# A recurrent layer between two feed-forward layers: POOL's normalisation ahead of inject, TensorE's gates ahead of the next transposes, and a negated mean that is added

## The chip, the cores and the metric

The kernel runs on one core of a Trainium2 chip. The metric is the device time in microseconds of one execution. The engines are named as in the profile: PE (TensorE, the matrix engine; PEld are its weight loads), DVE (VectorE), ACT (ScalarE), POOL (GpSimd) and SP, which only issues DMAs here.

## The reference

The input x has 32 x 256 rows of 128 features. Three layers follow, each with a layer norm and a residual:

```python
def _layernorm(x, axis=-1, eps=1e-05):
    m = jnp.mean(x, axis=axis, keepdims=True)
    v = jnp.var(x, axis=axis, keepdims=True)
    return (x - m) / jnp.sqrt(v + eps)
...
x = x + 0.5 * _L0_ffn_ref(_layernorm(x, axis=-1), L0_ffn_w_up, L0_ffn_w_down)
x = x + _L0_attn_ref(_layernorm(x, axis=-1), L0_attn_Wf, L0_attn_Wi, L0_attn_Wh)
x = x + 0.5 * _L0_ffn_ref(_layernorm(x, axis=-1), L0_ffn_w_up, L0_ffn_w_down)
```

The FFN is two linear layers with weights of -1, 0 and 1 (128 to 512 features and back) with a gelu between them; each divides its input by its root mean square first. The middle layer is a gated recurrence over the 256 positions of a sequence: with f and i the sigmoids of x Wf and x Wi, and g a positive function of x Wh, it computes h[t] = f[t] h[t-1] + i[t] g[t] from h = 0.5, in the reference by way of logarithms and an associative scan.

## The kernel before

The 8192 rows are held in SBUF as `X`, 64 tiles of 128 rows, and worked on in 16 groups of four tiles. The three layers run one after the other, each over the 16 groups, so there are 48 group steps, n = 0 to 47: n below 16 is the first FFN, 16 to 31 the recurrent layer, 32 to 47 the second FFN. Every engine has one queue with an order written out by hand, and semaphores between them. An instruction that waits holds up all that stands behind it on its engine.

**Each group of each layer begins alike.** DVE computes mean and variance of the rows (`stats`, `mean_var`, into `mv`). POOL makes the scale: for an FFN in `ln_roots`, for two groups at a time (L176 and L178 two small tensor_scalars, L180 a square root as a power, L183 an add), of which DVE takes the reciprocal `rstd` (L500); for the recurrent layer in `rnn_scales` (L188, L191), one group at a time. Then POOL's `norm` (L201) writes the normalised rows to `xn` with four instructions of 128x128: subtract the mean, multiply by rstd, both of them per-partition scalars. `xn` has two buffers; `norm(n)` waits until group n-2 is transposed. TensorE's `turn(n)` (L333) transposes the four tiles into the one PSUM buffer `T`, and waits until T was taken for the group before.

**FFN.** ACT and DVE take T apart into two float16 halves `xt_hi` (L259) and `xt_lo` (L504). TensorE multiplies with the up weights (L351, L352), ACT applies gelu (L263) and makes `h_hi` (L269), DVE makes `h_lo` (L508) and `h_half` (L516). `gram` (L368, L373, L374) gives the sums of squares on a diagonal, which DVE reads out as `ssq` (L521); POOL's `rms_step` (L208, L211) makes the root of it; DVE takes the reciprocal (`scale_y`, L525) and `add_ffn` (L532) adds the down product `Y` (L386) to X.

**Recurrent layer**, group r (n = 16 + r). ACT copies T to `xt` (`copy_turned`, L275; two buffers). `gates(r)` on TensorE (L401) makes three products of 512 columns in float32, each of them two records in the trace. ACT's `gate(r, n)` (L282) applies the sigmoid to each: `sig_h`, `sig_i`, and f in place. DVE's `candidate` (L540) makes `cand` from the first, POOL's `inject_step` (L219) multiplies it by sig_i, DVE's `scan` (L550) runs the recurrence into `hidden`, TensorE's `turn_back` (L410) transposes that into PSUM, and DVE's `add_rnn` (L556) adds it to X. The queues are ordered by a step s, which on POOL and DVE goes over all layers, with r = s - 16:

- POOL in step s: inject(r), rnn_scales(s - 12), norm(s + 2), then ln_roots and rms_step where there are any
- DVE in step s: scan(r - 1), candidate(r), stats and mean_var for the second FFN of group r - 2 and for the recurrent layer of group s - 11, add_rnn(r - 1)
- ACT in step r: the copy of group r + 1, then the three sigmoids of group r
- TensorE in step r: turn of group r + 1, gates(r), turn_back(r - 1)

Of the kernel before, what the change touches and what calls it, by code (L numbers as in the profile page):

```python
# [8 lines left out]
ALU = mybir.AluOpType  # L9
# [3 lines left out]
P = 128  # L13
# [9 lines left out]
def build_macaron(nc, x_in, w_f, w_i, w_h, w_up, w_down, x_out):  # L23
# [3 lines left out]
    tiles = batch * seq // P  # L27
    groups = tiles // TILES
# [7 lines left out]
    with ExitStack() as ctx:  # L36
        def sb(name, shape, dt=F32):
            return ctx.enter_context(nc.sbuf_tensor(name, shape, dt))
# [22 lines left out]

        st = sb("st", [P, 3, 2, TILES, 6])
        mv = [sb(f"mv{l}", [P, tiles, 2]) for l in range(3)]
        rstd = [sb(f"rstd{l}", [P, tiles]) for l in range(3)]
        var_eps = [sb(f"var_eps{l}", [P, 2, 4 * TILES]) for l in range(3)]
        root = [sb(f"root{l}", [P, 2, 4 * TILES]) for l in range(3)]
# [56 lines left out]
        def cols(g, n=TILES):  # L123
            return slice(g * TILES, g * TILES + n)
# [26 lines left out]
        @block.gpsimd  # L151
        def _(pool):
            eng = nc.gpsimd
            eng.memset(ident[:], 0.0).then_inc(ident_zero, 1)
            eng.memset(ones[:], 1.0).then_inc(consts_set, 1)
            eng.memset(half[:], 0.5).then_inc(consts_set, 1)
            eng.memset(minus_half[:], -0.5).then_inc(consts_set, 1)
            pool.wait_ge(ident_zero, 1)
            eng.affine_select(out=ident[:], in_=ident[:], compare_op=ALU.not_equal, fill=1.0, base=0,
                              pattern=[[-1, P]], channel_multiplier=1).then_inc(consts_set, 1)  # L160

            def gram_constants():
                eng.memset(ident16[:], 0.0).then_inc(ident_zero, 1)
                eng.memset(off_diag[:], OFF_DIAGONAL).then_inc(ident_zero, 1)
                pool.wait_ge(ident_zero, 3)
                eng.affine_select(out=ident16[:], in_=ident16[:], compare_op=ALU.not_equal, fill=1.0, base=0,
                                  pattern=[[-1, P]], channel_multiplier=1).then_inc(consts_set, 1)
                eng.affine_select(out=off_diag[:], in_=off_diag[:], compare_op=ALU.not_equal, fill=0.0, base=0,
                                  pattern=[[0, TILES], [-1, P]], channel_multiplier=1).then_inc(consts_set, 1)

            def ln_roots(i, l, first, n):

                w, par, s = n * TILES, i % 2, XN_SPLIT ** -2
                var = mv[l][:, cols(first, w), 1]
                pool.wait_ge(mv_done[l], i + 1)
                eng.tensor_scalar(var_eps[l][:, par, 0:w], var, s * RMS_EPS ** 2, LN_EPS * s * RMS_EPS ** 2,  # L176
                                  ALU.mult, ALU.add).then_inc(var_set[l], 1)
                eng.tensor_scalar(var_eps[l][:, par, w:2 * w], var, s, 1.0, ALU.mult, ALU.mult).then_inc(var_set[l], 1)  # L178
                pool.wait_ge(var_set[l], 2 * (i + 1))
                eng.tensor_tensor(root[l][:, par, 0:2 * w], var_eps[l][:, par, 0:2 * w], half[:, 0:2 * w],  # L180
                                  ALU.pow).then_inc(root_done[l], 1)
                pool.wait_ge(root_done[l], i + 1)
                eng.tensor_tensor(den[l][:, par, 0:w], root[l][:, par, 0:w], root[l][:, par, w:2 * w],  # L183
                                  ALU.add).then_inc(den_done[l], 1)

            def rnn_scales(g):
                pool.wait_ge(mv_done[1], g + 1)
                eng.tensor_scalar(var_eps[1][:, g % 2, 0:TILES], mv[1][:, cols(g), 1], 1.0, LN_EPS,  # L188
                                  ALU.mult, ALU.add).then_inc(var_set[1], 1)
                pool.wait_ge(var_set[1], g + 1)  # L190
                eng.tensor_tensor(rstd[1][:, cols(g)], var_eps[1][:, g % 2, 0:TILES], minus_half[:],  # L191
                                  ALU.pow).then_inc(rstd_done[1], 1)

            def norm(n):
                l, g = divmod(n, groups)
                pool.wait_ge(rstd_done[l], link_of(l, g) + 1)
                if n >= 2:
                    pool.wait_ge(xt_ready, n - 1)
                for t in range(TILES):
                    c = g * TILES + t  # L200
                    m = eng.tensor_scalar(xn[:, n % 2, t, :], X[:, c, :], mv[l][:, c, 0:1], rstd[l][:, c:c + 1],  # L201
                                          ALU.subtract, ALU.mult)
                m.then_inc(xn_ready, 1)

            def rms_step(F):
                par = F % 2
                pool.wait_ge(ssq_done, F + 1)
                eng.tensor_tensor(rms[:, par, :], ssq[:, par, :], half[:, 0:TILES], ALU.pow).then_inc(rms_ready, 1)  # L208
                pool.wait_ge(rms_ready, F + 1)

                eng.tensor_scalar(rms_den[:, par, :], rms[:, par, :], 2.0 * (2.0 / dff) ** 0.5, 2.0 * H_SPLIT * RMS_EPS,  # L211
                                  ALU.mult, ALU.add).then_inc(rms_den_done, 1)

            def inject_step(g):
                pool.wait_ge(cand_done, g + 1)
                pool.wait_ge(sig_done, 3 * g + 2)
                if g >= 2:
                    pool.wait_ge(scan_done, g - 1)
                eng.tensor_tensor(inject[:, g % 2, :], sig_i[:, g % 2, :], cand[:, g % 2, :], ALU.mult).then_inc(inject_done, 1)  # L219

            ln_roots(0, *links(0)[0])
            norm(0)
            ln_roots(1, *links(0)[1])
            gram_constants()
            norm(1)
            ln_roots(2, *links(0)[2])
            for s in range(0, 3 * groups):
                k, r, q = s, s - groups, s - 2 * groups
                if 0 <= r < groups:
                    inject_step(r)  # L230
                if 0 <= s - 12 < groups:
                    rnn_scales(s - 12)
                if s + 2 < 3 * groups:
                    norm(s + 2)
                if k + 4 < groups and k % 2 == 1:
                    ln_roots(link_of(0, k + 3), *links(0)[link_of(0, k + 3)])
                if 0 <= s - 28 < groups and s % 2 == 0:
                    ln_roots((s - 28) // 2, *links(2)[(s - 28) // 2])
                if 0 <= k - 1 < groups:
                    rms_step(k - 1)  # L240
                if 0 <= q - 1 < groups:
                    rms_step(q - 1 + groups)
            rms_step(2 * groups - 1)

        @block.scalar
        def _(act):
            eng = nc.scalar
# [29 lines left out]
            def gate(g, n):  # L277
                act.wait_ge(gate_ready, 3 * g + n + 1)
                if n == 1 and g >= 2:
                    act.wait_ge(inject_done, g - 1)  # L280
                out = (sig_h[:, g % 2, :], sig_i[:, g % 2, :], Z[g % 2][2])[n]
                eng.activation(out, Z[g % 2][n], ACT.Sigmoid).then_inc(sig_done, 1)  # L282
# [23 lines left out]
                ffn(k, k + 1)  # L306
            act.preload_act_table(ACT.Sigmoid)
            for r in range(groups):
                if r + 1 < groups:
                    turned(groups + r + 1)  # L310
                for n in range(3):
                    gate(r, n)
            act.preload_act_table(ACT.Gelu)
            turned(2 * groups)
            for k in range(groups):
# [3 lines left out]
        def _(pe):  # L319
# [8 lines left out]
            def turn(n):  # L328
                pe.wait_ge(xn_ready, n + 1)
                if n >= 1:  # L330
                    pe.wait_ge(xt_taken, n)
                for t in range(TILES):
                    m = pe.transpose(T[:, t * P:(t + 1) * P], xn[:, n % 2, t, :], ident[:])  # L333
                m.then_inc(xt_ready, 1)
# [68 lines left out]
            def turn_back(g):  # L403
                pe.wait_ge(scan_done, g + 1)
                if g == 0:
                    pe.wait_ge(ssq_done, groups)
                else:
                    pe.wait_ge(rnn_added, g)
                for t in range(TILES):
                    m = pe.transpose(O[:, t, :], hidden[:, g % 2, t * P:(t + 1) * P], ident[:])  # L410
                m.then_inc(turned_back, 1)
# [20 lines left out]
            gram(groups - 1)  # L432
            down(groups - 1)
            for r in range(groups):
                turn(groups + r + 1)
                gates(r)
                if r >= 1:
                    turn_back(r - 1)
            up(groups, 0)
            turn(2 * groups + 1)  # L440
            up(groups, 1)
# [192 lines left out]
```

## Time and profile before

| | |
|---|---|
| median of 3 runs | 420.42 us (419.04 to 420.66) |
| the profiled execution | 420.15 us, span 417.7 us |
| mean granted TensorE clock | 0.894 of full speed |
| POOL busy | 292.7 us (70%), 385 instructions |
| PE busy | 293.7 us (70%), 2701 matmuls |
| DVE busy | 276.3 us (66%) |
| ACT busy | 183.9 us (44%) |

The span runs from the first to the last instruction; what lies around it makes up the rest of the execution's time. A busy share is an average over the three layers, so the stages have to be read apart. Matmuls overlap one another in the records: their starts, not the sum of their lengths, tell how fast they went. Times in a timeline are in microseconds from the start of the span. A row with "xN" has merged N like instructions that followed one another.

### The profile page before, as it was taken

Reading aid. Unit: us, or ns where it says so; the run is one execution under the profiler, and the core shown is the slowest. Engines: PE = TensorE matmul, PEld = TensorE weight load, DVE = VectorE, ACT = ScalarE, POOL = GpSimd, SP = SyncE. Lnnn points to the kernel's source line nnn. Section 1 sums busy time; section 2 is a strip of 40 time slices with the busy share of each in tenths; the row PEclk is TensorE's granted clock in tenths of the full one; section 3 lists DMA queues with packets and bytes.
Section 4 is the critical chain, followed back from the end, with each engine's and each line's share of the span. In section 5 each row is a group of like instructions: output and inputs, shape, how many; then the busy total and the mean of one; then the engine's idle time right before and its main releaser. Section 6 shows DMA issues by size and latency. Waiting matters only on the chain. (4 is left out here: it accounts for less than half of the span.)

```text
span 417.7 us, 7376 instructions
## 1 busy us (share of the span) xinstructions
PE 293.7 (70%) x2701; PEld 205.5 (49%) x2701; DVE 276.3 (66%) x827; ACT 183.9 (44%) x230; POOL 292.7 (70%) x385
## 2 busy tenths in 40 slices
PE   1549988998898445555446555455679889888994
PEld 1228776777677222222223222222258668666874
DVE  5469999999898254444444443242578977887995
ACT  1257757575655212222222222222386656665670
POOL 4997988898896655545554445575798889888722
PEclk9969999999999786678886668877799999999999
DMA  6900000000000000000000000000000101110111
GB/s 200 271 0 2 2 2 3 2 2 2 2 2 2 0 2 0 0 0 0 2 1 0 1 0 0 0 0 0 3 0 27 52 27 31 48 52 27 53 52 50
DMA packets 18035, 9.57 MB, mean 23 GB/s; under 512 B 592, under 2 KB 17872, under 8 KB 18000
## 3 DMA queue, kind: packets, MB, share of 16 engines
q1 hardware_dynamic: 16896, 8.39, 7.3%
q10 hardware_dynamic: 1104, 0.72, 0.6%
q8 instruction: 21, 0.34, 0.3%
q14 instruction: 14, 0.11, 0.1%
HBM read 4.92 MB, written 4.19 MB: 22 GB/s over the span
## 5 line engine op out<-in xcount | busy, mean ns | idle before, releaser
L201 POOL TENSOR_SCALAR xn<-X,mv,rstd 128x128 f32<-128x128 f32 x192 | 152.5, 808 | 3.0 <-DVE rstd L500 0.9
L263 ACT ACTIVATE U<-U 128x1024 f32<-128x1024 f32 x64 | 65.6, 1025 | 79.5 <-PE U L352 79.5
L333 PE MATMUL T<-ident,xn 128*128 128x128 f32 x192 | 37.8, 331 | 77.3 <-POOL xn L201 77.3
L508 DVE SCALAR_TENSOR_TENSOR h_lo<-U,h_hi 128x1024 f16<-128x1024 f32 x64 | 77.6, 1213 | 1.9 <-ACT h_hi L269 1.9
L219 POOL TENSOR_TENSOR inject<-sig_i,cand 128x512 f32<-128x512 f32 x16 | 20.3, 1268 | 74.1 <-DVE cand L540 38.1
L351 PE MATMUL U<-xt_hi,up_w 128*128 128x512 f16 x128 | 51.0, 398 | 29.7 <-DVE h_lo L508 23.3
L333 PEld LDWEIGHTS T<-ident,xn 128*128 128x128 f32 x192 | 27.3, 168 | 90.4 <-POOL xn L201 85.1
L269 ACT ACTIVATE h_hi<-U 128x1024 f16<-128x1024 f32 x64 | 65.9, 1030 | 1.0
L540 DVE SCALAR_TENSOR_TENSOR cand<-U,sig_h 128x512 f32<-128x512 f32 x16 | 11.0, 686 | 76.2 <-ACT sig_h L282 76.2
L386 PE MATMUL Y<-down_w,h_hi 128*128 128x128 f16 x512 | 60.6, 219 | 0.0
L386 PE MATMUL Y<-down_w,h_lo 128*128 128x128 f16 x512 | 60.6, 219 | 0.0
L374 PE MATMUL G<-h_lo,h_hi 128*128 128x128 f16 x512 | 60.6, 219 | 0.0
L373 PE MATMUL G<-h_half,h_hi 128*128 128x128 f16 x512 | 60.6, 219 | 0.0
L374 PEld LDWEIGHTS G<-h_lo,h_hi 128*128 128x128 f16 x512 | 50.1, 98 | 3.8
L373 PEld LDWEIGHTS G<-h_half,h_hi 128*128 128x128 f16 x512 | 50.1, 98 | 3.4
L208 POOL TENSOR_TENSOR rms<-ssq,half 128x4 f32<-128x4 f32 x32 | 32.7, 1021 | 25.9 <-DVE ssq L521 25.9
L352 PE MATMUL U<-xt_lo,up_w 128*128 128x512 f16 x128 | 50.5, 394 | 0.0
L386 PEld LDWEIGHTS Y<-down_w,h_lo 128*128 128x128 f16 x512 | 50.1, 98 | 0.0
L386 PEld LDWEIGHTS Y<-down_w,h_hi 128*128 128x128 f16 x512 | 50.1, 98 | 0.0
L275 ACT COPY xt<-T 128x512 f32<-128x512 f32 x16 | 9.4, 587 | 89.4 <-PE T L333 89.4
L180 POOL TENSOR_TENSOR root<-var_eps,half 128x16 f32<-128x16 f32 (+1 forms) x17 | 47.3, 2782 | 1.4
L401 PE MATMUL U<-xt,gate_w 128*128 128x512 f32 x64 | 48.1, 895 | 0.0
(66 smaller groups left out, 416.5 us busy)
## 6 DMA issues: line engine op xcount, KB each, us to landing
X<-in_L_attn_x SPq DMA_DIRECT2D x16, 256.0 KB, 5.2
out_x<-X SPq DMA_DIRECT2D x16, 256.0 KB, 2.3
up_raw<-in_L_ffn_w_up ACTq DMA_DIRECT2D x1, 256.0 KB, 4.1
down_raw<-in_L_ffn_w_down ACTq DMA_DIRECT2D x1, 256.0 KB, 4.9
gate_raw<-in_L_attn_Wh ACTq DMA_DIRECT2D x1, 64.0 KB, 4.5
gate_raw<-in_L_attn_Wi ACTq DMA_DIRECT2D x1, 64.0 KB, 4.3
gate_raw<-in_L_attn_Wf ACTq DMA_DIRECT2D x1, 64.0 KB, 4.2
```

The lines of the kernel that those rows point to most:

```text
L180: eng.tensor_tensor(root[l][:, par, 0:2 * w], var_eps[l][:, par, 0:2 * w], half[:, 0:2 * w], ALU.pow).then_inc(root_done[l], 1)
L201: m = eng.tensor_scalar(xn[:, n % 2, t, :], X[:, c, :], mv[l][:, c, 0:1], rstd[l][:, c:c + 1], ALU.subtract, ALU.mult)
L263: eng.activation(U[part][:], U[part][:], ACT.Gelu, scale=1.0 / XN_SPLIT).then_inc(gelu_done, 1)
L269: eng.mul(h_hi[:, F % 2, 2 * part:2 * part + 2, :], U[part][:], H_SPLIT).then_inc(h_hi_done, 1)
L333: m = pe.transpose(T[:, t * P:(t + 1) * P], xn[:, n % 2, t, :], ident[:])
L351: pe.matmul(U[part][:, c, :], up_w[:, f0:f0 + P], xt_hi[:, F % 2, :], start=True, stop=False)
L352: m = pe.matmul(U[part][:, c, :], up_w[:, f0:f0 + P], xt_lo[:, F % 2, :], start=False, stop=True)
L373: pe.matmul(G[:, t, :], hi, half_, start=False, stop=False)
L374: m = pe.matmul(G[:, t, :], hi, lo, start=False, stop=(t == TILES - 1 and c == chunks - 1))
L386: m = pe.matmul(Y[:, par, t, :], part[:, par, c, t * P:(t + 1) * P], down_w[:, c, :], start=(c == 0 and part is h_hi), stop=(c == chunks - ...
L401: pe.matmul(Z[g % 2][n], gate_w[:, n, :], xt[:, g % 2, :], start=True, stop=True).then_inc(gate_ready, 1)
L508: vec.scalar_tensor_tensor(out=h_lo[:, F % 2, 2 * part:2 * part + 2, :], in0=U[part][:], scalar=H_SPLIT, in1=h_hi[:, F % 2, 2 * part:2 * p ...
```

## The change

Three things change. First, for every group of every layer POOL computes the negated mean into a new buffer `neg_mean` with one more small tensor_scalar (in `ln_roots` and in `rnn_scales`), and `norm` adds it instead of subtracting the mean; the number it waits for on `var_set` rises accordingly. Second, in POOL's loop norm(s + 2) comes first in a step, ahead of inject_step and rnn_scales. Third, in the recurrent layer TensorE issues gates(r) and turn_back(r - 1) ahead of the turn of group r + 1, and ACT issues the three sigmoids of group r ahead of the copy of group r + 1.

```diff
--- before.py
+++ after.py
@@ -61,6 +61,7 @@
 
         st = sb("st", [P, 3, 2, TILES, 6])
         mv = [sb(f"mv{l}", [P, tiles, 2]) for l in range(3)]
+        neg_mean = [sb(f"neg_mean{l}", [P, tiles]) for l in range(3)]
         rstd = [sb(f"rstd{l}", [P, tiles]) for l in range(3)]
         var_eps = [sb(f"var_eps{l}", [P, 2, 4 * TILES]) for l in range(3)]
         root = [sb(f"root{l}", [P, 2, 4 * TILES]) for l in range(3)]
@@ -176,7 +177,9 @@
                 eng.tensor_scalar(var_eps[l][:, par, 0:w], var, s * RMS_EPS ** 2, LN_EPS * s * RMS_EPS ** 2,
                                   ALU.mult, ALU.add).then_inc(var_set[l], 1)
                 eng.tensor_scalar(var_eps[l][:, par, w:2 * w], var, s, 1.0, ALU.mult, ALU.mult).then_inc(var_set[l], 1)
-                pool.wait_ge(var_set[l], 2 * (i + 1))
+                eng.tensor_scalar(neg_mean[l][:, cols(first, w)], mv[l][:, cols(first, w), 0], -1.0, 1.0,
+                                  ALU.mult, ALU.mult).then_inc(var_set[l], 1)
+                pool.wait_ge(var_set[l], 3 * (i + 1))
                 eng.tensor_tensor(root[l][:, par, 0:2 * w], var_eps[l][:, par, 0:2 * w], half[:, 0:2 * w],
                                   ALU.pow).then_inc(root_done[l], 1)
                 pool.wait_ge(root_done[l], i + 1)
@@ -187,7 +190,9 @@
                 pool.wait_ge(mv_done[1], g + 1)
                 eng.tensor_scalar(var_eps[1][:, g % 2, 0:TILES], mv[1][:, cols(g), 1], 1.0, LN_EPS,
                                   ALU.mult, ALU.add).then_inc(var_set[1], 1)
-                pool.wait_ge(var_set[1], g + 1)
+                eng.tensor_scalar(neg_mean[1][:, cols(g)], mv[1][:, cols(g), 0], -1.0, 1.0,
+                                  ALU.mult, ALU.mult).then_inc(var_set[1], 1)
+                pool.wait_ge(var_set[1], 2 * (g + 1))
                 eng.tensor_tensor(rstd[1][:, cols(g)], var_eps[1][:, g % 2, 0:TILES], minus_half[:],
                                   ALU.pow).then_inc(rstd_done[1], 1)
 
@@ -198,8 +203,8 @@
                     pool.wait_ge(xt_ready, n - 1)
                 for t in range(TILES):
                     c = g * TILES + t
-                    m = eng.tensor_scalar(xn[:, n % 2, t, :], X[:, c, :], mv[l][:, c, 0:1], rstd[l][:, c:c + 1],
-                                          ALU.subtract, ALU.mult)
+                    m = eng.tensor_scalar(xn[:, n % 2, t, :], X[:, c, :], neg_mean[l][:, c:c + 1], rstd[l][:, c:c + 1],
+                                          ALU.add, ALU.mult)
                 m.then_inc(xn_ready, 1)
 
             def rms_step(F):
@@ -226,12 +231,12 @@
             ln_roots(2, *links(0)[2])
             for s in range(0, 3 * groups):
                 k, r, q = s, s - groups, s - 2 * groups
+                if s + 2 < 3 * groups:
+                    norm(s + 2)
                 if 0 <= r < groups:
                     inject_step(r)
                 if 0 <= s - 12 < groups:
                     rnn_scales(s - 12)
-                if s + 2 < 3 * groups:
-                    norm(s + 2)
                 if k + 4 < groups and k % 2 == 1:
                     ln_roots(link_of(0, k + 3), *links(0)[link_of(0, k + 3)])
                 if 0 <= s - 28 < groups and s % 2 == 0:
@@ -306,10 +311,10 @@
                 ffn(k, k + 1)
             act.preload_act_table(ACT.Sigmoid)
             for r in range(groups):
+                for n in range(3):
+                    gate(r, n)
                 if r + 1 < groups:
                     turned(groups + r + 1)
-                for n in range(3):
-                    gate(r, n)
             act.preload_act_table(ACT.Gelu)
             turned(2 * groups)
             for k in range(groups):
@@ -432,10 +437,10 @@
             gram(groups - 1)
             down(groups - 1)
             for r in range(groups):
-                turn(groups + r + 1)
                 gates(r)
                 if r >= 1:
                     turn_back(r - 1)
+                turn(groups + r + 1)
             up(groups, 0)
             turn(2 * groups + 1)
             up(groups, 1)
```

## Rows read from the trace of the kernel before

**Rows 1.** Windows: width, busy us (xinstructions) of PE PEld DVE ACT POOL, PEclk, DMA, GB/s

```profile
36.00:132.00 96.00, 86.17 (x1079) 68.25 (x1078) 90.93 (x266) 62.82 (x71) 84.00 (x112) 1.00 0.01 2
139.00:300.00 161.00, 85.03 (x210) 42.93 (x210) 66.76 (x265) 36.59 (x61) 89.61 (x110) 0.76 0.00 0
...
220.00:224.00 4.00, 3.73 (x8) 2.18 (x9) 0.24 (x1) 1.18 (x2) 0.22 (x1) 0.50 0.00 0
```

**Rows 2.** Timeline, POOL: start us, us, engine, line, operation, out<-in, [idle before <-releaser]

```profile
138.87 1.27 POOL L219 TENSOR_TENSOR inject<-sig_i,cand 128x512 f32<-128x512 f32 x1 [5.57 <-ACT sig_i L282]
...
204.08 1.27 POOL L219 TENSOR_TENSOR inject<-sig_i,cand 128x512 f32<-128x512 f32 x1 [4.64 <-DVE cand L540]
205.44 0.19 POOL L188 TENSOR_SCALAR var_eps<-mv 128x4 f32<-128x4 f32 x1
205.72 1.03 POOL L191 TENSOR_TENSOR rstd<-var_eps,minus_half 128x4 f32<-128x4 f32 x1
206.74 3.13 POOL L201 TENSOR_SCALAR xn<-X,mv,rstd 128x128 f32<-128x128 f32 x4
...
299.16 1.26 POOL L219 TENSOR_TENSOR inject<-sig_i,cand 128x512 f32<-128x512 f32 x1 [2.07 <-DVE cand L540]
```

**Rows 3.** Timeline, TensorE and ACT in one period

```profile
220.27 1.11 PE L333 MATMUL T<-ident,xn 128*128 128x128 f32 x4 [5.33 <-POOL xn L201]
...
221.18 5.32 PE L401 MATMUL U<-xt,gate_w 128*128 128x512 f32 x6
221.42 0.59 ACT L275 COPY xt<-T 128x512 f32<-128x512 f32 x1 [6.30 <-PE T L333]
```

**Rows 4.** Waits, 150 to 280 us: waiter <- releaser: total us, times, longest

```profile
PE T L333 <- POOL xn L201: 60.5, 12, 5.6
```

**Rows 5.** POOL's groups by form: count | busy us, mean ns | idle before

```profile
L201 POOL TENSOR_SCALAR xn<-X,mv,rstd 128x128 f32<-128x128 f32 x192 | 152.5, 808 | 3.0 <-DVE rstd L500 0.9
L180 POOL TENSOR_TENSOR root<-var_eps,half 128x16 f32<-128x16 f32 x15 | 44.0, 2931 | 1.2
...
L178 POOL TENSOR_SCALAR var_eps<-mv 128x8 f32<-128x8 f32 x15 | 3.0, 202 | 1.3
...
L178 POOL TENSOR_SCALAR var_eps<-mv 128x4 f32<-128x4 f32 x2 | 0.4, 204 | 0.2
...
L159 POOL TENSOR_SCALAR_AFFINE_SELECT ident<-ident 128x128 f32<-128x128 f32 x1 | 0.3, 296 | 0.0
```

**Rows 6.** Timeline, POOL in the first FFN

```profile
34.99 1.01 POOL L208 TENSOR_TENSOR rms<-ssq,half 128x4 f32<-128x4 f32 x1 [0.55 <-DVE ssq L521]
...
131.99 1.03 POOL L208 TENSOR_TENSOR rms<-ssq,half 128x4 f32<-128x4 f32 x1
```

**Rows 7.** Timeline, DVE at the start, in the first FFN and behind it

```profile
23.62 0.20 DVE L500 RECIPROCAL rstd<-den 128x8 f32<-128x8 f32 x1 [4.57 <-POOL den L183]
...
120.50 0.15 DVE L525 RECIPROCAL y_scale<-rms_den 128x4 f32<-128x4 f32 x1
...
127.04 0.14 DVE L525 RECIPROCAL y_scale<-rms_den 128x4 f32<-128x4 f32 x1
...
145.97 0.18 DVE L525 RECIPROCAL y_scale<-rms_den 128x4 f32<-128x4 f32 x1 [5.59 <-POOL rms_den L211]
```

**Rows 8.** The chain that ended last, second FFN: start us, us, what

```profile
314.63 1.03 POOL rms L208
...
370.73 1.03 POOL rms L208
...
388.90 1.79 PE Y L386 x32
...
394.85 1.79 PE Y L386 x32
```

**Rows 9.** Timeline, DVE in the recurrent layer

```profile
202.99 0.69 DVE L540 SCALAR_TENSOR_TENSOR cand<-U,sig_h 128x512 f32<-128x512 f32 x1 [5.83 <-ACT sig_h L282]
...
206.53 1.26 DVE L550 TENSOR_TENSOR_SCAN hidden<-U,inject 128x256 f32<-128x256 f32 x2
```

## The prediction

> **What bounds the kernel now.** I read the profile in five steps.
>
> First the windows [rows 1]. In the first FFN (36 to 132 us) TensorE is busy 90% and its granted clock is 1.00. In the recurrent layer (139 to 300) no engine is busy above 56%, and the granted clock averages 0.76, a mixture of its two levels, 1.2 and 2.4 GHz. A stage of 161 us in which nothing is full is a ring of waits.
>
> Second, the ring, in the timeline [rows 2, 3]. POOL multiplies `inject` at 204.08, makes the scales, starts `norm` at 206.74 and ends it at 209.87. One period on, TensorE, idle for 5.33 us, transposes at 220.27 right behind the last normalised tile, and only then issues the gates, whose input was copied a period before. The waits put 60.5 us in 12 periods on this pair [rows 4]. The gates release the sigmoid, that the candidate, that POOL's next inject. So a period is POOL's 2.66 + 3.13, the turn's 0.91, then gate, sigmoid and candidate, one after the other. First inject 138.87, last 299.16: 15 periods in 160.3 us, 10.7 each.
>
> Third, POOL's groups by form [rows 5]: one xn instruction (128x128, two operations) is 808 ns, and 192 of them make 152.5 of POOL's 292.7 us.
>
> Fourth, the first FFN: rms of group 0 at 34.99, of group 14 at 131.99 [rows 6], 6.93 a group. DVE in a step without a wait goes from 120.50 to 127.04 [rows 7], 6.54; with rstd's 0.20 in every other one it needs 6.6. So what POOL costs there is 0.33 a group.
>
> Fifth, the chain in the second FFN [rows 8]: rms at 314.63 and, eight groups on, at 370.73 is 7.01 a group, through POOL's roots, norm and rms. Later, with the norms nearly over, the chain is TensorE's, from 388.90 to 394.85, 5.95 a group.
>
> **The change, part by part.**
>
> *The order.* TensorE now issues gates(r), turn_back(r-1), then the turn of group r+1; ACT its three sigmoids, then the copy; POOL norm, then inject and scales. xn has two buffers, and norm of recurrent group r+2 needs only the turn of group r, so norm stands no longer between one group's inject and the next group's gates. What is added is a bubble on TensorE: the copy now lies between a turn and the gates behind it. Cycles that remain, per group:
> - TensorE at 1.2 GHz: gates 6 x 0.85 = 5.12 (5.32 with the last one's tail), turn 0.91 (220.27 to 221.18), turn_back as much, 6.94. The bubble is the turn's tail 0.20, the copy 0.59 and 0.1 of handovers [rows 3]: 0.9. Sum 7.85. At 2.4 GHz the work is half, 3.47, and the sum 4.35.
> - POOL: 2.66 + 3.13 = 5.79, with the negation 6.07 (norm as now).
> - DVE: candidate 202.99 to scans 206.53, 3.54, and the scans' 1.2: 4.75 [rows 9].
> - Scan, turn_back, turn, copy, gate, sigmoid, candidate, inject, scan: about 7 at 2.4 GHz (1.2 + 0.5 + 0.5 + 0.8 + 1.0 + 0.7 + 0.7 + 1.4), but from one group to the next but one, so 3.5 each.
>
> Which clock? At 1.2 GHz TensorE would work 6.94 of 7.85 us, 88%, as densely as in the FFN where 1.00 is granted. At 2.4 GHz its holes would be 1 to 2 us, between the 0.7 per group of the FFN and today's 5.3. I take 2.4 GHz nearly throughout.
>
> *POOL's queue at the ends.* At s = 16 norm(18) goes ahead of inject(0); what it awaits, the turn of 16, is over by then. Behind inject and scales stands rms of group 15, for which DVE (scale_y, ahead of scan(0)) waits 5.59 us today [rows 7]. It comes 3.1 us earlier: a first period of about 7. At s = 30 norm(32) goes ahead of inject(14); the rstd that it awaits is made at s = 28. No DMA moves; SP's stores await ffn_added as now.
>
> *The negated mean.* One small tensor_scalar in each of 17 ln_roots and 16 rnn_scales: 0.20, or 0.28 with the gap (205.44 to 205.72). In the second FFN, where POOL's roots are in the loop, 0.28 a pair of groups.
>
> *Add for subtract in xn.* Not in the trace. Upper end: 808 ns, the instruction as it is. Lower end: 296 ns, affine_select with one input and one output of 128x128 f32. Between: the inject multiply has two inputs and takes 1.27 us at 128x512; less a fixed 0.20 that is 2.1 ns an element, so 467 at 128. The small rows [rows 5] speak for the low end: multiply-multiply takes 202 ns at 8 columns and 204 at 4, no slope, where subtract-multiply, with the same fixed part, has 4.7 ns a column and would show 19. But they have constants, and xn has per-partition scalars. I take 350 ns: a norm of 1.4 for 3.13.
>
> The Trainium skill, GPSIMD Engine Reference, section 4.1, says that one-input elementwise work on POOL goes at roughly line rate. The 808 ns of now does not agree. By its rule, with the 1.2 GHz of section 1, 128 columns are 107 ns over the fixed part, an estimate of 0.31 us, and the sum would come out 1 us lower than with my 350.
>
> **The sum**, against the profiled execution's 420.15 us (span 417.7; the runs' median is 420.42, so it is the same):
> - start: norm(0) stands ahead of roots(1), norm(1) ahead of roots(2), and DVE idles for their result until 23.62 [rows 7]: 2 x 1.9, less 0.5 of negations: -3.3
> - first FFN: 14 x (6.93 - 6.6) = -4.6; the negation hides behind DVE, and if it did not it would be +2
> - recurrent: with norm at 1.4 POOL needs 4.34, TensorE 4.35, DVE 4.75; I add 0.15 of handovers. 7 + 14 x 4.9 = 75.6 for 160.3: -84.7
> - into the second FFN (300 to 315): two norms out of the way, a warm clock: -3, of which I know only the sign
> - second FFN: TensorE needs 5.95. In the step with roots POOL needs 1.45 + 4.0 (the root row's 2.93, four small ones and gaps) + 1.4 = 6.9 and delays DVE's scale_y, so 6.2: 10 x (7.01 - 6.2) = -8.1
>
> Together -103.7: **316.5 us**.
>
> **Rivals.**
> 1. *Add is no faster than subtract*; the per-partition scalars are what is slow. Recurrent layer bound by POOL, 7 + 14 x 6.15 = 93: -67; transition -1; negations in the FFNs and at the start +3.4. Sum about -64: 356. For it: the small rows use constants. Against: their missing slope. Chance 0.20.
> 2. *The clock falls back.* Fast xn, but 1.2 GHz in the whole recurrent layer: 7 + 14 x 7.85 = 117, -43, the rest -19: 358. With half the groups at either level 337. For it: today's 0.76, and 0.50 at 220 to 224 us behind a hole of 5.33 [rows 1]. Against: 1.00 in the FFN with small holes. Chance 0.13. The Trainium skill, TensorE: Matmul & The Clock Gate, Part 1, says that an idle array goes to 1.2 GHz and that sustained work lifts it to 2.4; those rows agree.
> 3. *The ring closes anew*, the slower side. If norm had to await the same group's turn, inject stood behind it and TensorE awaited both, a period at 1.2 GHz would be norm 3.13, inject and scales 2.94, scan 1.2, turn_back and turn 1.8, copy 0.9, first gate 1.7, sigmoid and candidate 1.3: 13.0, so 15 x 2.3 = +35: 455. It decides once a period exceeds 10.7. Against: xn, xt, cand and inject all have two buffers. Chance 0.02.
> 4. *DVE couples worse.* Its order puts two stats between candidate and add, and its scan then waits for inject: 5.8 a group instead of 4.9, 14 x 0.9 = 13 more: 329. Chance 0.15.
>
> My forecast itself, 307 to 326, has the other 0.50.
>
> **Numbers.** The likeliest case gives 316.5. The range goes from 306 (xn at 296 ns, 4.5 a group, second FFN at 6.0) to 359, which takes in rivals 1, 2 and 4; a slow xn and a slow clock together would lie above it, at 380. A measurement of this kernel can tell about 0.5% from no change. Faster 0.96, same 0.01, slower 0.03 (rival 3, and as much again for what I have not seen).
>
> **What would show it.** After: the mean of xn (350 or 808) decides between the forecast and rival 1. TensorE's wait of T on xn, 60.5 us now, is near nothing in the recurrent layer. First to last inject is 75 us, with DVE nearly full; 93 with POOL full if rival 1 holds; 117 with TensorE full at 0.50 if rival 2 does. Rms to rms is 6.6 in the first FFN and 6.2 in the second. I am wrong above all if xn is no faster, or if holes of 1 to 2 us are enough to lower the clock.

## The result, and the profile after

The changed kernel takes 325.73 us (median of 4 runs, 325.29 to 326.07) against 419.73 for the kernel before beside it: a ratio of 0.776, interval 0.773 to 0.779. I had forecast 316.5 us with a range of 306 to 359. The profiled execution's span is 324.3 us, 93.4 below before's 417.7.

From the page's first two parts, after: busy us of each engine, then tenths of DVE's busy share and of the granted clock in 40 slices:

```profile
PE 268.9 (83%) x2701; PEld 194.0 (60%) x2701; DVE 273.4 (84%) x827; ACT 183.4 (57%) x230; POOL 230.7 (71%) x418
...
DVE  4458999999999998488999985389988988989993
...
PEclk9996999999999999969999999879999999999999
```

DVE's row stands at 8 and 9 nearly throughout; the granted clock's row has a 6 at the start (4th slice), another in the 18th (about 138 to 146 us) and 8 and 7 in the 26th and 27th (203 to 219 us). The windows of the same stages as in [rows 1] (columns as there), first FFN, recurrent layer, second FFN:

```profile
33.00:125.00 92.00, 86.74 (x1105) 69.65 (x1102) 90.65 (x265) 62.56 (x71) 66.75 (x122) 1.00 0.01 2
132.00:214.00 82.00, 63.27 (x216) 31.21 (x213) 66.04 (x266) 37.83 (x64) 71.13 (x124) 0.94 0.00 1
...
228.00:300.00 72.00, 69.42 (x872) 55.79 (x870) 63.84 (x134) 49.96 (x58) 54.38 (x97) 1.00 0.15 42
```

The recurrent layer has 82 us in place of 161, DVE and POOL are busy 81 and 87% of it, and the granted clock is 0.94 instead of 0.76.

POOL's groups by form, which answer to [rows 5]:

```profile
L206 POOL TENSOR_SCALAR xn<-X,neg_mean,rstd 128x128 f32<-128x128 f32 x192 | 84.1, 452 | 3.6 <-DVE rstd L505 0.9
...
L193 POOL TENSOR_SCALAR neg_mean<-mv 128x4 f32<-128x4 f32 x16 | 3.1, 194 | 1.4
...
L180 POOL TENSOR_SCALAR neg_mean<-mv 128x8 f32<-128x8 f32 x15 | 3.0, 197 | 0.0
```

xn went from 808 to 452 ns. Then the ring. POOL's timeline from the first inject to the last (answering to [rows 2]), with one period in the middle:

```profile
132.37 1.26 POOL L224 TENSOR_TENSOR inject<-sig_i,cand 128x512 f32<-128x512 f32 x1 [4.72 <-ACT sig_i L287]
...
160.31 1.27 POOL L224 TENSOR_TENSOR inject<-sig_i,cand 128x512 f32<-128x512 f32 x1
161.67 0.19 POOL L191 TENSOR_SCALAR var_eps<-mv 128x4 f32<-128x4 f32 x1
161.94 0.19 POOL L193 TENSOR_SCALAR neg_mean<-mv 128x4 f32<-128x4 f32 x1
162.22 1.02 POOL L196 TENSOR_TENSOR rstd<-var_eps,minus_half 128x4 f32<-128x4 f32 x1
163.24 1.74 POOL L206 TENSOR_SCALAR xn<-X,neg_mean,rstd 128x128 f32<-128x128 f32 x4
164.94 1.27 POOL L224 TENSOR_TENSOR inject<-sig_i,cand 128x512 f32<-128x512 f32 x1
...
174.34 1.27 POOL L224 TENSOR_TENSOR inject<-sig_i,cand 128x512 f32<-128x512 f32 x1
...
179.03 1.26 POOL L224 TENSOR_TENSOR inject<-sig_i,cand 128x512 f32<-128x512 f32 x1
...
193.06 1.27 POOL L224 TENSOR_TENSOR inject<-sig_i,cand 128x512 f32<-128x512 f32 x1
...
213.11 1.26 POOL L224 TENSOR_TENSOR inject<-sig_i,cand 128x512 f32<-128x512 f32 x1 [0.35 <-DVE cand L545]
```

First to last is 80.7 us, where it was 160.3. A period is 4.63 us at 160.31 and 4.69 at 174.34, and inject has no wait behind the last xn: at 160.31 POOL goes on without a gap. TensorE in the same period, answering to [rows 3]:

```profile
160.19 0.60 PE L338 MATMUL T<-ident,xn 128*128 128x128 f32 x4
...
160.82 0.59 ACT L280 COPY xt<-T 128x512 f32<-128x512 f32 x1 [0.29 <-PE T L338]
...
161.46 2.84 PE L406 MATMUL U<-xt,gate_w 128*128 128x512 f32 x6 [0.68 <-ACT xt L280]
```

The 5.33 us that the transposes waited for xn are gone. What stands in front of the gates now is 0.68 us for the copy, as reckoned (0.59 and 0.1 of handovers). The chain that ended last runs through DVE alone here. In the kernel before, that view reaches back only to 281 us, and there it goes through POOL, TensorE and ACT in turn. After:

```profile
159.58 0.58 DVE cand L545
...
163.09 1.18 DVE hidden L555 x2
164.27 0.58 DVE cand L545
```

Candidate to candidate is 4.69 us (159.58 to 164.27). POOL's own round is 4.63 to 4.64: it goes at that pace from 151 to 165 us, catching up after a late start, and then falls in with DVE's 4.69 to 4.70. So DVE sets the pace of the steady part, with POOL only 0.06 us a round under it.

**Where the 93.4 us came from**, by marks that both traces have (POOL's rms and inject, all in microseconds):

| stretch | before | after | gain | forecast |
|---|---|---|---|---|
| start to rms of group 0 | 34.99 | 33.49 | 1.5 | 3.3 |
| to rms of group 14 | 97.00 | 90.89 | 6.1 | 4.6 |
| to inject(0) | 6.88 | 7.99 | -1.1 | 0 |
| to inject(15) | 160.29 | 80.74 | 79.6 | 84.7 |
| to rms of group 16 | 15.47 | 14.90 | 0.6 | 3 |
| ten groups more | 70.12 | 63.34 | 6.8 | 8.1 |
| rest | 32.95 | 32.95 | 0 | 0 |

### The profile page after: what moved, and what is told of

Read it like the earlier page. It is cut to its first block, busy times and chain, and to the rows that moved or that the text cites. A ratio compares the mean times of both kernels' runs of the same rounds, so it can differ in the third digit from the quotient of the medians.

```text
span 324.3 us, 7409 instructions
## 1 busy us (share of the span) xinstructions
PE 268.9 (83%) x2701; PEld 194.0 (60%) x2701; DVE 273.4 (84%) x827; ACT 183.4 (57%) x230; POOL 230.7 (71%) x418
## 4 chain that ended last, share of the span: by engine, by line
DVE 47%; POOL 24%; PE 15%; issue 8%; ACT 3%; DMA 1%; POOLq 0%; DVEq 0%; ACTq 0%
DVE h_lo L513 9%; POOL root L183 9%; DVE st L492 8%; DVE X L537 6%; POOL xn L206 5%; POOL rms L213 4%; DVE ssq L526 4%; DVE h_half L521 4%; PE U L406 4%; DVE hidden L555 4%; DVE xt_lo L509 4%; DVE mv L498 3%; PE Y L391 2%; DVE cand L545 2%; PE U L356 2%
## 5 line engine op out<-in xcount | busy, mean ns | idle before, releaser
L206 POOL TENSOR_SCALAR xn<-X,neg_mean,rstd 128x128 f32<-128x128 f32 x192 | 84.1, 452 | 3.6 <-DVE rstd L505 0.9
L492 DVE BATCH_NORM_STATS2 st<-X 128x6 f32<-128x128 f32 x192 | 40.9, 276 | 4.6 <-DMA X<-in_L_attn_x 4.6
L406 PE MATMUL U<-xt,gate_w 128*128 128x512 f32 x64 | 35.6, 685 | 10.2 <-ACT xt L280 10.2
L537 DVE SCALAR_TENSOR_TENSOR X<-Y,y_scale,X 128x128 f32<-128x128 f32 x128 | 36.1, 345 | 1.1
L356 PEld LDWEIGHTS U<-xt_hi,up_w 128*128 128x128 f16 x128 | 12.9, 100 | 34.2 <-DVE h_lo L513 12.0
L338 PE MATMUL T<-ident,xn 128*128 128x128 f32 x192 | 31.2, 288 | 0.1
L338 PEld LDWEIGHTS T<-ident,xn 128*128 128x128 f32 x192 | 25.2, 149 | 7.8 <-issue 1.9
```

The source lines that it names most:

```text
L206: m = eng.tensor_scalar(xn[:, n % 2, t, :], X[:, c, :], neg_mean[l][:, c:c + 1], rstd[l][:, c:c + 1], ALU.add, ALU.mult)
L356: pe.matmul(U[part][:, c, :], up_w[:, f0:f0 + P], xt_hi[:, F % 2, :], start=True, stop=False)
L492: m = vec.bn_stats(st[:, l, g % 2, t, :], X[:, g * TILES + t, :])
L537: m = vec.scalar_tensor_tensor(out=xt_, in0=Y[:, F % 2, t, :], scalar=y_scale[:, F % 2, t:t + 1], in1=xt_, op0=ALU.mult, op1=ALU.add)
```

## The experiments

The expectations were written with the changed kernel's trace at hand, so its FFN and start gains are in them.

**The two parts, each alone.** The first has the three reorderings without the negated mean, the second the negated mean with the old order. The edit of the second, against the changed kernel (the first is its complement):

```diff
@@ POOL
-                if s + 2 < 3 * groups:
-                    norm(s + 2)
                 if 0 <= r < groups:
                     inject_step(r)
                 if 0 <= s - 12 < groups:
                     rnn_scales(s - 12)
+                if s + 2 < 3 * groups:
+                    norm(s + 2)
@@ ACT
+                if r + 1 < groups:
+                    turned(groups + r + 1)
                 for n in range(3):
                     gate(r, n)
-                if r + 1 < groups:
-                    turned(groups + r + 1)
@@ TensorE
+                turn(groups + r + 1)
                 gates(r)
                 if r >= 1:
                     turn_back(r - 1)
-                turn(groups + r + 1)
```

> The kernel before with the changed order on POOL, ACT and TensorE, but the mean subtracted as before and no negated mean. My theory: the order opens the ring and the slow xn then makes POOL the bound of the recurrent layer, 5.8 us a group and 8 in the last steps with ln_roots, first to last inject about 92 us, 352 us in all. Rival, the clock: with TensorE idle for over 2 us in each period it falls back to 1.2 GHz, and TensorE takes 7.85 us a group: about 377 us. Rival, the order is worth little without the faster xn: over 400.

> The negated mean and the add, with the order of before. My theory: the ring stays, each of its 15 periods is shorter by 1.39 less 0.28 for the negation, 17 us, and the start and the FFNs give the 14 us that the changed kernel shows there: about 388 us, with xn at 452 ns. Rival, the add is what opened the recurrent layer: under 345.

Measured: order alone 350.78 us, ratio 0.836 (0.832 to 0.839); add alone 388.53, ratio 0.926 (0.923 to 0.929). Both are at their theories' numbers, and the rivals of both are out. The order alone is worth 68 us, the add alone about 31, together 94: once the order has opened the ring, POOL bounds the layer, and the faster xn is worth 25 us more. POOL with the order alone:

```profile
163.09 1.28 POOL L219 TENSOR_TENSOR inject<-sig_i,cand 128x512 f32<-128x512 f32 x1
...
168.85 1.27 POOL L219 TENSOR_TENSOR inject<-sig_i,cand 128x512 f32<-128x512 f32 x1
```

5.76 us a period, inject with no wait in front: the 2.66 + 3.13 of [rows 2], one behind the other. And TensorE's clock in it, in a window (columns as in [rows 1]):

```profile
165.00:169.00 4.00, 2.60 (x12) 1.64 (x13) 3.93 (x20) 1.12 (x3) 4.00 (x6) 1.00 0.00 0
```

TensorE has holes of 0.68 and 1.15 us in each of these periods. From 148 to 202 us the clock stays at 1.00 with them; then, with no longer hole in front, it is at 0.50 for some 3.4 us:

```profile
202.60:206.00 3.40, 3.40 (x6) 1.32 (x4) 1.30 (x3) 1.19 (x2) 3.23 (x5) 0.50 0.00 0
```

POOL's period there stays at 5.76. In the run with the old order it is at 0.898 over the span, as before (0.894).

**Is each half of the reordering needed?** The changed kernel with one half taken back: TensorE and ACT as in the diff above (e3), or POOL as in it (e4).

> The changed kernel with TensorE's and ACT's old order (turn of group r+1, then gates(r); copy, then sigmoids); POOL's norm still ahead of inject. Theory A: either half of the reordering opens the ring, since xn of group r+1 is ready when TensorE comes to it, and the copy now hides behind the gates, so the 0.68 us hole in front of the gates goes: DVE stays the bound, 322 to 327 us. Theory B: both halves are needed, since the gates stand behind a turn again: about 388, as with the old order everywhere.

> The changed kernel with POOL's old order (inject, scales, then norm); TensorE's and ACT's new order stay. Theory A (either half opens the ring): gates(r) no longer await norm of group r+1, and POOL's 4.7 us a group go on without a ring: 325 to 330 us. Theory B (both are needed): about 388.

Measured: 324.03 us (ratio 0.773, 0.770 to 0.775) with POOL's half alone, 331.65 (0.791, 0.788 to 0.793) with TensorE's and ACT's alone. Theory A stands for both: one half opens the ring, at least with the fast xn; no run tried one half with the slow one. The second figure lies a little over its 325 to 330. POOL's half is the better one, and the other adds nothing to it (325.73 with both, if anything 1.7 more). That difference isn't in the steady part, which goes at 4.63 to 4.70 us in both, but mostly in the second and third periods, 4.6 and 4.6 with POOL's half alone for 6.2 and 5.1. With TensorE's half alone, POOL's queue in the last steps is inject, norm, ln_roots, so the roots that DVE waits for come a norm later (it waits 6.04 and 5.76 us for them, where the changed kernel waits 4.53 and 4.05), and the last three periods are 9.1, 6.5 and 9.1 us:

```profile
193.82 1.27 POOL L224 TENSOR_TENSOR inject<-sig_i,cand 128x512 f32<-128x512 f32 x1
...
202.89 1.27 POOL L224 TENSOR_TENSOR inject<-sig_i,cand 128x512 f32<-128x512 f32 x1 [2.07 <-DVE cand L545]
...
209.38 1.27 POOL L224 TENSOR_TENSOR inject<-sig_i,cand 128x512 f32<-128x512 f32 x1 [3.50 <-issue]
...
218.43 1.26 POOL L224 TENSOR_TENSOR inject<-sig_i,cand 128x512 f32<-128x512 f32 x1 [2.07 <-DVE cand L545]
```

**What makes xn fast.** Four forms in one kernel, one per tile of a group, and two more copies of the mean:

```diff
+                    if t == 0:
+                        eng.tensor_scalar(xn[:, n % 2, t, lo], X[:, c, lo], neg_mean[l][:, c:c + 1], rstd[l][:, c:c + 1],
+                                          ALU.add, ALU.mult)
...
+                    elif t == 1:
+                        eng.tensor_scalar(xn[:, n % 2, t, lo], X[:, c, lo], mv[l][:, c, 0:1], rstd[l][:, c:c + 1],
+                                          ALU.subtract, ALU.mult)
...
+                    elif t == 2:
+                        m = eng.tensor_scalar(xn[:, n % 2, t, :], X[:, c, :], mean_c[l][:, c:c + 1], rstd[l][:, c:c + 1],
+                                              ALU.subtract, ALU.mult)
+                    else:
+                        m = eng.tensor_scalar(xn[:, n % 2, t, :], X[:, c, :], neg2[l][:, c, 0:1], rstd[l][:, c:c + 1],
+                                              ALU.add, ALU.mult)
```

(`lo` is the first 64 columns; a second instruction of the same form, left out here, does the other 64.)

> The changed kernel with four forms of the normalising instruction, one per tile of a group, and two more small copies of the mean: tile 0 adds the negated mean in two halves of 64 columns, tile 1 subtracts the mean in two halves, tile 2 subtracts a mean that lies without gaps (as neg_mean does), tile 3 adds a negated mean that lies with a gap of one (as mv does). Theory: the operation alone makes the speed, so tile 2 takes about 800 ns and tile 3 about 450. Rival: where the scalar lies makes it; then tile 2 takes 450 and tile 3 800. The halves give the price of a column: with a fixed part of 200 ns, 64 columns take about 320 added and 500 subtracted. Only the durations matter here.

POOL's groups by form in that kernel:

```profile
L228 POOL TENSOR_SCALAR xn<-X,mean_c,rstd 128x128 f32<-128x128 f32 x48 | 39.0, 812 | 0.0
...
L223 POOL TENSOR_SCALAR xn<-X,mv,rstd 128x64 f32<-128x64 f32 x48 | 28.5, 594 | 0.0
...
L231 POOL TENSOR_SCALAR xn<-X,neg,rstd 128x128 f32<-128x128 f32 x48 | 21.5, 447 | 0.0
...
L220 POOL TENSOR_SCALAR xn<-X,neg_mean,rstd 128x64 f32<-128x64 f32 x48 | 19.3, 402 | 0.0
```

The operation alone makes the speed: subtract out of the dense buffer 812 ns, add out of the gapped one 447. The halves: add 402 and 447, so 0.7 ns a column on a fixed 0.36 us; subtract 594 and 812, 3.4 ns a column on a fixed 0.38. The halves were expected at 320 and 500, with a fixed part of 0.20; that part was too low. This kernel's total tells nothing.

**Where the last periods lose time.** In steps 28 and 30 there is a wait in DVE's step of [rows 9]. DVE after:

```profile
198.37 0.20 DVE L505 RECIPROCAL rstd<-den 128x8 f32<-128x8 f32 x1 [4.53 <-POOL den L186]
198.49 1.26 DVE L555 TENSOR_TENSOR_SCAN hidden<-U,inject 128x256 f32<-128x256 f32 x2
...
211.06 0.20 DVE L505 RECIPROCAL rstd<-den 128x8 f32<-128x8 f32 x1 [4.05 <-POOL den L186]
```

DVE stands in `scales` for POOL's roots, 4.53 and 4.05 us, ahead of scans 12 and 14.

```diff
-                if 0 <= s - 28 < groups and s % 2 == 0:
-                    scales((s - 28) // 2, *links(2)[(s - 28) // 2])
+                if 0 <= s - 29 < groups and s % 2 == 1:
+                    scales((s - 29) // 2, *links(2)[(s - 29) // 2])
```

> The changed kernel with DVE's reciprocal for the second FFN (scales) one step later in its queue, so that it no longer waits for POOL's roots ahead of scan(12) and scan(14). Theory: those two waits of 4.5 and 4.1 us are what made the last three periods 20.0 us in place of 14.1; POOL with its roots then sets 6.9 + 3.0 a pair, so the last three periods are about 16.5: 322 us. Rival: POOL's roots between two injects set these periods anyway, no change from 325.7.

Measured 321.05 us (0.765, 0.762 to 0.768), a gain of 4.7. The last three periods take 17.2 us (192.78 to 209.94) for 20.1: the wait was 2.9 us of it, and POOL's roots between two injects are the rest of what these periods have over 4.7 each (7.0, 3.2 and 7.0). Another 1.3 us of the gain lies between the last inject and rms of group 16 (13.6 us for 14.9). The rival falls.

**Where the first periods lose time.** After the first gates TensorE waits for add_ffn(15), and its clock falls:

```profile
134.59 1.02 PE L406 MATMUL Y<-xt,gate_w 128*128 128x512 f32 x2
137.98 1.13 PE L406 MATMUL Y<-xt,gate_w 128*128 128x512 f32 x2 [2.38 <-DVE X L537]
...
141.39 5.35 PE L406 MATMUL U<-xt,gate_w 128*128 128x512 f32 x6 [0.68 <-ACT xt L280]
```

```profile
141.00:145.00 4.00, 3.61 (x5) 1.54 (x6) 2.50 (x6) 0.94 (x2) 3.18 (x8) 0.50 0.01 2
```

Behind the hole of 2.38 us six gate records take 5.35 us, against 2.84 at 2.4 GHz. The edit brings rms(15) forward:

```diff
 # POOL
                     norm(s + 2)
+                if s == groups:
+                    rms_step(groups - 1)
                 if 0 <= r < groups:
                     inject_step(r)
...
-                if 0 <= k - 1 < groups:
+                if 0 <= k - 1 < groups - 1:
                     rms_step(k - 1)
 # DVE
+                if r == 0:
+                    sum_squares(groups - 1)
                 if 0 <= r < groups:
                     candidate(r)
...
-                    if 0 <= j < groups:
+                    if 0 <= j < groups and s != groups:
                         sum_squares(E)
```

> The changed kernel with the sum of squares of group 15 ahead of the first candidate on DVE, and its rms ahead of the first inject on POOL. Theory: scan(0) and the two later gates of group 1, which wait for add_ffn(15) until 137.9 us, start up to 4 us earlier, and TensorE's hole of 2.4 us in front of them goes, and with it the stretch at 1.2 GHz from 140 to 146 us: 320 to 322 us. Rival: something else follows closely behind, 324 to 326.

Measured 322.06 us (0.767, 0.764 to 0.770), 3.7 less. The first three periods are 4.6 each, 13.9 us for 18.7, and the clock is 1.00 from the start; the last three are 1.2 us longer than in the changed kernel. Of the 4.8 us some 2.8 are the first period's wait for add_ffn(15) (7.4 us, with or without a stretch at 1.2 GHz behind it), the other 2.0 the clock:

```profile
132.47 1.27 POOL L224 TENSOR_TENSOR inject<-sig_i,cand 128x512 f32<-128x512 f32 x1 [2.21 <-ACT sig_i L289]
...
137.10 1.27 POOL L224 TENSOR_TENSOR inject<-sig_i,cand 128x512 f32<-128x512 f32 x1
```

```profile
141.00:145.00 4.00, 3.33 (x14) 1.79 (x13) 3.93 (x18) 2.23 (x4) 3.74 (x7) 1.00 0.00 0
```

**What the negation costs, and what a cheaper xn would give.** The first leaves the negation out (norm adds the mean itself; the edit is shown for rnn_scales, that of ln_roots and norm is of the same kind), the second leaves out the normalisation of one tile of four:

```diff
-                eng.tensor_scalar(neg_mean[1][:, cols(g)], mv[1][:, cols(g), 0], -1.0, 1.0,
-                                  ALU.mult, ALU.mult).then_inc(var_set[1], 1)
-                pool.wait_ge(var_set[1], 2 * (g + 1))
+                pool.wait_ge(var_set[1], g + 1)
```

```diff
+                    if t == 3 and n >= 2:
+                        continue
```

> The changed kernel without the negation: norm adds the mean itself out of mv, so the negated mean is left out of the computation. Theory: xn stays at 450 ns; the negation costs 0.28 us in each of five pairs of the second FFN, 0.15 at each of three roots at the start and in the two roots of the recurrent layer, and nothing in the first FFN and the rest of the recurrent layer, where DVE is the bound: 2 us less than the changed kernel's 325.7, about 323.5. Rival: POOL is the bound of the recurrent layer, 15 x 0.28 more: 319.5.

> The changed kernel with norm writing three of a group's four tiles from group 2 on; the fourth tile's normalisation is left out. norm then takes 1.3 us in place of 1.74, what it would take with xn at 330 ns. It tells how much of the 9 us by which the forecast was too low comes from xn's price (435 ns a step for my 350). Theory: little, since DVE bounds the first FFN and the recurrent layer: 0.4 in each pair of the second FFN, 0.4 in each of the last recurrent pairs and as much at the start, about 322. Rival: POOL is what sets the pace almost everywhere now, 15 x 0.4 more: 316.

Measured 322.17 us (0.767, 0.765 to 0.769) and 322.18 (0.767, 0.764 to 0.769). Both are near their theories' totals, but in part by luck: in neither is there the stretch at 1.2 GHz. TensorE's hole for add_ffn(15) is 2.10 us without the negation, and the next gates go at full speed. With three tiles the hole is 2.38 us, as in the changed kernel, and the clock is 1.00 behind it all the same.

```profile
137.13 1.12 PE L401 MATMUL Y<-xt,gate_w 128*128 128x512 f32 x2 [2.10 <-DVE X L532]
...
140.07 2.41 PE L401 MATMUL U<-xt,gate_w 128*128 128x512 f32 x5 [0.68 <-ACT xt L275]
```

With three tiles, TensorE and a window (columns as in [rows 1]):

```profile
138.34 1.12 PE L408 MATMUL Y<-xt,gate_w 128*128 128x512 f32 x2 [2.38 <-DVE X L539]
```

```profile
139.00:143.00 4.00, 3.27 (x14) 1.72 (x13) 3.95 (x13) 1.72 (x3) 2.61 (x4) 1.00 0.01 2
```

Of the 3.5 us that the negation seems to cost, 2.9 lie in the first three periods (15.8 for 18.7): some 2.0 of them are this clock, the rest 0.28 a period and the instruction's. In the steady part the period is 4.70 us with and without it, so POOL is not what bounds there, and the second FFN is nearly the same (63.1 us in ten groups for 63.3). With three tiles the second FFN goes at 6.19 us a group for 6.33, 1.5 us in ten groups, and the steady periods stay at 4.70. The rivals of both, in which POOL sets the pace, fall.

**All of it together.** POOL's half of the order, late scales, early rms, and ln_roots of the second FFN for single groups from group 4 on; and the same without the single groups. The edit of the single groups (DVE's scales follow in the same way, one step later):

```diff
-                    2: [(l, g, 2) for g in range(0, groups, 2)]}[l]
+                    2: [(l, 0, 2), (l, 2, 2)] + [(l, g, 1) for g in range(4, groups)]}[l]
...
-                if 0 <= s - 28 < groups and s % 2 == 0:
-                    ln_roots((s - 28) // 2, *links(2)[(s - 28) // 2])
+                for i, link in enumerate(links(2)):
+                    if s - 28 == link[1]:
+                        ln_roots(i, *link)
```

> POOL's new order with TensorE's and ACT's old one (324.0 us alone), the late scales, the early rms of group 15, and ln_roots of the second FFN for one group at a time from its group 4 on, so that POOL's steps there are even: 5.9 us each instead of 7.2 and 3.3. Theory: the gains add, -4 for the scales, -3 for the rms (the stretch at 1.2 GHz is gone already), and the second FFN goes at TensorE's 5.95 a group in place of 6.3, -3: 313 to 315 us. Rival: the smaller roots cost POOL more than they even out: 317 or more.

> The combined kernel without its ln_roots for single groups, so POOL's new order, TensorE's and ACT's old one, late scales, early rms of group 15. Theory: the second FFN goes at 6.3 us a group again in place of 5.95, 3 us over the combined kernel's 314.7: 317.5. Rival: the single roots gained nothing: 314.7.

Measured 314.69 us (0.751, 0.747 to 0.754) and 318.40 (0.759, 0.756 to 0.761). The combined kernel is the fastest of the study, 25% under the kernel before and 11 us under the changed one. POOL's rms in its second FFN:

```profile
227.62 1.20 POOL L213 TENSOR_TENSOR rms<-ssq,half 128x4 f32<-128x4 f32 x1
...
233.62 1.16 POOL L213 TENSOR_TENSOR rms<-ssq,half 128x4 f32<-128x4 f32 x1
...
239.56 1.16 POOL L213 TENSOR_TENSOR rms<-ssq,half 128x4 f32<-128x4 f32 x1
```

5.95 to 6.0 a group, which is TensorE's pace of [rows 8], where the same kernel with pairs takes 6.36. The smaller roots (1.66 us for one group, 2.9 for two) cost POOL more in all and lose nothing in this stage, where its steps are even now. They do lose ahead of it: the last three periods of the recurrent layer take 19.3 us with them for 17.2 with pairs, and the way from the last inject to rms of group 16 another 1.1. So the medians give the theory's 3 us, as 3.7, but by stages the traces show 4.0 gained in ten groups and some 3 lost before. The two traces can't settle the rest: that of the pairs is the shortest of its six executions (316.06 us of 316.06 to 320.30, granted clock 0.987), that of the single groups the longest of its four (316.53 of 313.62 to 316.53, 0.973).

## Why the prediction was right

The measured 325.7 us lies in the range, and just inside the 307 to 326 that I gave to the forecast itself. The two big mechanisms came as told; the sizes were 10.3 us too hopeful, and all the larger misses but one went the same way.

**The ring and what opens it: right, and shown.** TensorE's wait on xn went from 5.33 us a period to nothing, first to last inject from 160.3 to 80.7, and the reordering alone gives 350.8 us with xn as slow as ever. What the working did not see is that either half of the reordering would do: I reckoned TensorE's bubble (0.9; 0.68 of it as a wait) as a price without asking whether POOL's half alone would do. It does, and is if anything 1.7 us faster, though the steady period is the same with and without the bubble. Rival 3, a ring that closes anew above 10.7 us a period, is out at 4.7.

**DVE as the next bound, 4.75: right.** It is 4.69 to 4.70, and the 0.15 for handovers was not needed. POOL, which I had at 4.34, needs 4.63 to 4.64: that DVE is still the bound is luck by 0.06 us, as a slightly dearer xn would have made it POOL. Rival 4 (5.8 us a group, 329 us in all) is nearer to the measured total than my 316.5, but its mechanism does not show: the steady period is 4.7.

**xn at 350 ns: mis-sized.** One xn step is 435 ns (1.74 in four; the record's mean 452). The slope was where I looked, and it is small for an add, 0.7 ns a column; the fixed part was my error. I gave the instruction the 0.20 us of the small rows in [rows 5], which have constants, and it is 0.36, for add and subtract alike. That the fixed part comes from the per-partition scalars I suppose; no run varied that. Rival 1, that add is no faster than subtract, is out. It cost little: with norm at 1.31 us the second FFN gives 0.3 a pair, 1.5 us in ten groups.

**The clock: right in the main, with rival 2 in small.** 1.00 through the steady part with holes of about 1 us, 0.50 from 139.7 to 146.4 us behind the hole of 2.38, and again at 201 to 204 behind one of 2.99 and at 215 to 218 behind holes of 2.26 and 1.86. The length of the last hole does not decide it: with three tiles the same 2.38 had no such stretch behind it, in the combined kernel with pairs not even a hole of 3.32 (1.00 from 194 to 202 us), and with the order alone 0.50 came at 202.6 with no hole over 1.15 in front. What does decide it stays open. The rule of the Trainium skill that I weighed (TensorE: Matmul & The Clock Gate, Part 1), that an idle array goes to 1.2 GHz and sustained work lifts it again, agrees with most of these rows in kind; the one at 202.6 it doesn't explain. The first three periods came out 1.9 us over my sum (18.7 for 16.8), which the early rms took away.

**The step that failed most:** "7 + 14 x 4.9". It priced all 14 periods by the row of a steady one. In three of them DVE stood behind POOL's roots: 20.1 us for 14.7, 5.4 over. I had POOL's root in the second FFN's loop and left it out here, though ln_roots runs at s = 28 and 30, and DVE's wait for it was in the trace before:

```profile
277.20 0.20 DVE L500 RECIPROCAL rstd<-den 128x8 f32<-128x8 f32 x1 [6.93 <-POOL den L183]
```

The late scales gave back 4.7 us in all, 2.9 of them in these three periods; the 2.5 that these still have over my 14.7 are POOL's roots themselves.

**Smaller terms.** The transition into the second FFN was -3 of which I knew "only the sign": -0.6. The warm clock that I had counted in was not there (0.50 at 215 to 218 us), and the chain that ended last goes through the first groups' own work on ACT, TensorE and DVE from 212 to 228 us, not through the norms. Inject(0) came 1.1 us later behind rms of group 14 than before, for which I had no term. The start gave 1.5 for 3.3: norm(0) took 2.30 and not 1.4, norm(1) began 0.64 earlier and not 2, and DVE got its rstd at 22.01 for 23.62 [rows 7]. The second FFN was 6.33 a group for my 6.2, the first 6.49 for 6.6: there POOL had cost more than the 0.33 a group that I read, so the stage gave 1.5 us more than forecast, which hides part of the other misses. The spans differ from the forecast by 10.3 us in all, the medians by 9.2.

**The negation.** I priced 0.28 an instruction; in ln_roots it adds 0.15, since it shares the gap of the one in front, and in rnn_scales 0.28. On the path it is worth some 2 us in all, a good half of it at the start and in the first three periods; in the steady part it is worth nothing, as forecast.

## What to carry to other kernels

When engines take turns and none is full, look for the one instruction that stands between a group's end and the next group's beginning only because of where it is in a queue; moving it past on one engine may be enough, and the second move gave nothing here. Price a stage by all its periods, not by its steady one: the steps with extra work (here the roots) and the first ones were most of what the forecast missed, 7.3 of 10.3 us. On POOL try the same arithmetic with an add before giving up an instruction as slow.

## What the runs showed of the hardware

- POOL's tensor_scalar on 128x128 float32 with two per-partition scalars takes 447 to 459 ns as add-multiply and 802 to 812 as subtract-multiply, 0.7 against 3.4 ns a column, wherever the scalar lies.
- With the order alone, TensorE's granted clock stayed at 1.00 for 54 us with holes of 0.68 and 1.15 us in each period of 5.76, and then was 0.50 for 3.4 us with the same holes. It fell to 0.50 behind single holes of 2.38 and 2.99 us in the changed kernel, but not behind one of 2.10 without the negation, one of 2.38 with three tiles, or one of 3.32 in the combined kernel with pairs. Where it fell behind the hole of 2.38, the next six gate records took 2.5 us more.
- In the start of the changed kernel one of POOL's small instructions took 0.71 us for 0.20, from 17.82, while DVE ran `down_t` (17.71 to 18.46), which reads two tensors in SBUF:

```profile
17.82 0.71 POOL L179 TENSOR_SCALAR var_eps<-mv 128x8 f32<-128x8 f32 x1
```

```profile
17.71 0.75 DVE L481 SCALAR_TENSOR_TENSOR down_t<-down_raw,limit,below 128x512 f32<-128x512 f32 x1
```

The Trainium skill, SBUF — State Buffer, section "Who interferes with whom", says that a DVE instruction with two SBUF inputs and a GpSimd instruction that reads SBUF exclude each other on a port that they share. The row agrees; no run here took the two apart.
